# A two-layer decoder on one core: small norm operations and Newton steps change engine, ternary weights are made in another layout, and some products are merged

## What is computed

```python
x = layernorm(x + decay_mix(x) + bias)                 # triangular decay matrix over 256 channels
x = layernorm(x + cross_attention(x, ctx))             # 16 heads, 64 context rows
x = layernorm(x + experts(x) + shared(x))              # top 1 of 8 experts
x = layernorm(x + spectral_attention(x))               # fft over heads, each normalised, cumulative sum
x = layernorm(x + latent_cross_attention(x, ctx))      # weights folded: Wq, w_kc_q, W_qr, W_kr; w_kc_kv, Wo
x = layernorm(x + ternary_ffn(x))                      # weights made ternary in groups of 64

def ternary_quant(w, g=64):
    w = w.astype(bfloat16); w_g = w.reshape(-1, g)
    scale = clip(mean(abs(w_g), -1), 1e-08)
    q = clip(round(w_g / scale), -1, 1)
    return w + ((q * scale).reshape(w.shape) - w)
```

## Time and profile before

| | |
|---|---|
| median of 3 runs | 691.98 us (689.49 to 692.77) |
| the profiled execution | 693.77 us, its span 692.5 us |
| instructions | 14605 |
| TensorE, VectorE, ScalarE, POOL busy | 590.3, 506.3, 406.3, 362.0 us |
| mean granted TensorE clock | 0.938 |

### The profile page before, as it was taken

The page is one execution under the profiler, slowest core; times in us unless marked ns, Lnnn a source line. Parts: engine busy times, 40 slices in busy tenths (PEclk is TensorE's granted clock), DMA queues, the critical chain, the costliest instruction groups (busy, mean ns, idle before and its releaser), DMA issues.

```text
span 692.5 us, 14605 instructions
## 1 busy us (share of the span) xinstructions
PE 590.3 (85%) x5393; PEld 456.3 (66%) x5393; DVE 506.3 (73%) x1297; ACT 406.3 (59%) x914; POOL 362.0 (52%) x405
## 2 busy tenths in 40 slices
PE   3899989889689999935448789999988999999995
PEld 3566867668566566622126578898666777878885
DVE  2675667668667666757999878678698998968475
ACT  2667756767665454624534637665855666577474
POOL 2255345364753003269899894635654544256465
PEclk9899999999999999965867999999998999999998
DMA  6753221110535432441101010001100010000001
GB/s 190 211 162 107 55 92 48 52 41 2 168 117 166 142 104 84 123 151 50 40 25 56 1 32 1 2 1 31 32 26 6 1 31 3 1 1 2 1 1 62
DMA packets 50416, 41.98 MB, mean 61 GB/s; under 512 B 15513, under 2 KB 48794, under 8 KB 50330
## 3 DMA queue, kind: packets, MB, share of 16 engines
q1 hardware_dynamic: 48810, 36.85, 17.9%
q0 software_dynamic: 1536, 4.20, 1.9%
HBM read 31.72 MB, written 10.35 MB: 61 GB/s over the span
## 4 chain that ended last, share of the span: by engine, by line
PE 55%; DVE 21%; ACT 8%; issue 5%; SPq 4%; DMA 4%; POOL 3%; DVEq 0%; POOLq 0%
PE bank L1032 8%; PE bank L1034 8%; PE bank L1033 8%; PE bank L1039 7%; PE bank L1453 6%; SPq L858 4%; PE bank L1217 2%; PE bank L1120 2%; PE bank L1106 2%; DVE wide L1766 2%; DMA wide<-in_L_ffn_down_w 2%; ACT first L1592 1%; PE bank L1129 1%; PE bank L1318 1%; DVE wide L1869 1%
## 5 line engine op out<-in xcount | busy, mean ns | idle before, releaser
L1766 DVE TENSOR_TENSOR first<-bank,first 128x512 f16<-128x512 f32 (+3 forms) x141 | 75.6, 556 | 23.3 <-ACT first L1601 9.8
L1039 PE MATMUL bank<-c_identity,first 128*128 128x128 f32 (+2 forms) x353 | 60.0, 285 | 23.5 <-DMA first<-in_x 9.8
L2223 POOL TENSOR_TENSOR first<-first 128x512 f16<-128x512 f32 x44 | 51.2, 1164 | 42.7 <-ACT first L1653 35.8
L1039 PEld LDWEIGHTS bank<-c_identity,first 128*128 128x128 f32 (+2 forms) x353 | 39.7, 140 | 35.0 <-ACT first L1592 10.3
L1032 PE MATMUL bank<-wide,first 128*128 128x256 f16 (+3 forms) x199 | 55.8, 290 | 4.5 <-DVE first L1766 2.1
L1039 PE MATMUL bank<-c_identity,wide 128*128 128x128 f32 (+3 forms) x211 | 36.6, 297 | 26.1 <-POOL wide L2311 9.0
L1033 PE MATMUL bank<-wide,first 128*128 128x256 f16 (+3 forms) x199 | 55.8, 290 | 0.0
L1034 PE MATMUL bank<-wide,first 128*128 128x256 f16 (+3 forms) x199 | 55.7, 290 | 0.0
L2203 POOL TENSOR_TENSOR first<-first,minus_half 128x2 f32<-128x2 f32 x30 | 22.2, 739 | 55.5 <-DVE first L1875 55.5
L1039 PEld LDWEIGHTS bank<-c_identity,wide 128*128 128x128 f32 (+3 forms) x211 | 24.7, 147 | 33.1 <-POOL wide L2311 10.1
L2258 POOL TENSOR_TENSOR wide<-wide 128x768 bf16<-128x768 bf16 x8 | 13.5, 1685 | 61.1 <-DVE wide L1862 61.0
(11 more groups left out here) (469 smaller groups left out, 2160.0 us busy)
## 6 DMA issues: line engine op xcount, KB each, us to landing
first<-sent_rows SPq DMA_DIRECT2D x20, 128.0 KB, 2.0
made_rows<-first SPq DMA_DIRECT2D x20, 128.0 KB, 1.9
wide<-in_L_xattn_Wq SPq DMA_DIRECT2D x9, 256.0 KB, 3.1
wide<-in_L_ffn_gate_w SPq DMA_DIRECT2D x8, 256.0 KB
wide<-in_L_ffn_up_w SPq DMA_DIRECT2D x8, 256.0 KB
wide<-in_L_ffn_down_w SPq DMA_DIRECT2D x8, 256.0 KB
wide<-in_L_xattn_Wo SPq DMA_DIRECT2D x16, 128.0 KB
wide<-in_L_ffn_w_gate_up SPq DMA_DIRECT2D x8, 256.0 KB
```

Source lines behind the costliest of these rows:

```text
L1039: last = nc.tensor.transpose(view[0:m, c0:c0 + n], src, kc["identity" if dt == F32 else "identity_bf"][0:n, 0:n])
L1766: return V.tensor_tensor(lo, whole, hi, ALU.subtract)
L2223: G.tensor_tensor(B.pl[r], B.pf, B.ph[r], ALU.subtract).then_inc(says("ex_l"), 1)
```

## The change

- `ln` keeps only the statistics. Minus the mean, variance plus eps, the pow and the shift are all on POOL in `ln_pow`; `ln_x` only applies them.
- `nr` keeps the two integer operations; a new part `nr_x` on POOL does the three Newton steps with four operations each.
- The ternary weights: `f_16` writes the two-byte copy with the 12 groups side by side (`of_groups`), so the group's scale is a repeated row of 12. `f_sc` has one operation less and makes two edges; `f_gt` compares with tensor_tensor and subtracts; `f_q` is one VectorE part of three operations, the last of which writes the original order.
- `hb` puts two heads in the two halves of the partitions and alternates them; `krT` is block diagonal over 128 rows, so `hc` has one product for two heads, and `hk` is one transpose. The bias is one product over 128 rows, two of which hold its high and low part. `ss` folds the two halves, so `rm` has half the products.
- The plan has new lengths and `settle` makes 30 passes instead of 8.

```diff
     def norm(u, n, rank, summed="res"):
-        p.add("ln", u, n, "DVE", 131, [(summed, u, n)], rank)
-        p.add("ln_pow", u, n, "POOL", 71, [("ln", u, n)], rank)
-        p.add("ln_x", u, n, "ACT", 120, [("ln_pow", u, n)], rank)
+        p.add("ln", u, n, "DVE", 108, [(summed, u, n)], rank)
+        p.add("ln_pow", u, n, "POOL", 95, [("ln", u, n)], rank)
+        p.add("ln_x", u, n, "ACT", 85, [("ln_pow", u, n)], rank)
...
-            p.add("f_sc", 0, i, "DVE", 160, [("f_16", 0, i)], rank)
-            p.add("f_gt", 0, i, "DVE", 183, [("f_sc", 0, i)], rank)
-            for n2 in range(4):
-                p.add("f_q", 0, 4 * i + n2, "POOL", 164, [("f_q", 0, 4 * i + n2 - 1) if n2 else ("f_gt", 0, i)], rank)
+            p.add("f_sc", 0, i, "DVE", 170, [("f_16", 0, i)], rank)
+            p.add("f_gt", 0, i, "DVE", 155, [("f_sc", 0, i)], rank)
+            p.add("f_q", 0, i, "DVE", 195, [("f_gt", 0, i)], rank)
...
-        p.add("nr", u, 0, "DVE", 355, [("ft_n", u, 0), ("ft_n", u, 1)], k)
-        p.add("nr_k", u, 0, "DVE", 81, [("nr", u, 0), ("ft_raw", u, 0), ("ft_raw", u, 1)], k)
-        p.add("nr_q", u, 0, "POOL", 106, [("nr", u, 0), ("ft_raw", u, 0), ("ft_raw", u, 1)], k + 0.1)
+        p.add("nr", u, 0, "DVE", 60, [("ft_n", u, 0), ("ft_n", u, 1)], k)
+        p.add("nr_x", u, 0, "POOL", 350, [("nr", u, 0)], k)
+        p.add("nr_k", u, 0, "DVE", 81, [("nr_x", u, 0), ("ft_raw", u, 0), ("ft_raw", u, 1)], k)
+        p.add("nr_q", u, 0, "POOL", 106, [("nr_x", u, 0), ("ft_raw", u, 0), ("ft_raw", u, 1)], k + 0.1)
...
-    p.settle(8, 8)
+    p.settle(8, 30)
...
-        flip(bank("hk", 0, j), [(n * DC, R, W.kr[:, n, :]) for n in range(HEADS)]).then_inc(says("hk"), 1)
+        flip(bank("hk", 0, j), [(0, P, W.kr.rearrange("p h n -> p (h n)"))]).then_inc(says("hk"), 1)
...
-        for n in range(HEADS):
-            for q in range(2):
-                last = mm(b[0:R, n * D:(n + 1) * D], W.qr[:, q, n, :], k.t1[:, n, q, :], start=(q == 0), stop=(q == 1))
+        for q in range(2):
+            for n in range(HEADS):
+                last = mm(b[n * R:(n + 1) * R, 0:D], W.qr[:, q, n, :], k.t1[:, n, q, :], start=(q == 0), stop=(q == 1))
...
-            for n in range(HEADS):
-                mm(b[:, (2 * c + n) * DC:(2 * c + n + 1) * DC], k.t2[:, n * D + c * P:n * D + (c + 1) * P], k.krT[:, n * DC:(n + 1) * DC],
-                   start=True, stop=True)
+            mm(b[:, c * P:(c + 1) * P], k.t2[:, c * P:(c + 1) * P], k.krT, start=True, stop=True)
...
-                    for half in range(2):
-                        last = mm(o, kc["all_ones"][0:1, :], k.bias[half], start=False, stop=(half == 1))
+                    last = mm(o, kc["all_ones"], k.bias, start=False, stop=True)
...
-            for n in range(2):
-                last = mm(b[:, t:t + 1], B.ss[:, n * S + t * P:n * S + (t + 1) * P], k.one, start=(n == 0), stop=(n == 1))
+            last = mm(b[:, t:t + 1], B.ss[:, t * P:(t + 1) * P], k.one, start=True, stop=True)
...
-        fn(W.w16, W.raw, ACT.Copy).then_inc(says("f_16"), 1)
+        fn(of_groups(W.w16), W.raw.rearrange("p (g n) -> p g n", n=GRP), ACT.Copy).then_inc(says("f_16"), 1)
...
-        for t in range(T):
-            last = fn(B.shift[:, t:t + 1], B.mean[:, t:t + 1], ACT.Copy, scale=B.rstd[:, t:t + 1])
-        act.step(last)
...
+        dve.step(V.tensor_reduce(W.sc32, of_groups(W.w16), AX.X, ALU.add, apply_absolute_value=True))
+        dve.step(V.tensor_scalar(W.sc16, W.sc32, 1.0 / GRP, 1e-8, ALU.mult, ALU.max))
+        for n in range(2):
+            last = V.tensor_scalar(W.edge[n], W.sc16, 0.5 - n, None, ALU.mult)
...
+        V.tensor_tensor(by_row(W.qa), by_row(W.w16), each_group(W.edge[0]), ALU.is_gt)
+        dve.step(V.tensor_tensor(by_row(W.qb), by_row(W.w16), each_group(W.edge[1]), ALU.is_lt))
+        V.tensor_tensor(W.qa, W.qa, W.qb, ALU.subtract).then_inc(says("f_gt"), 1)
...
+        dve.step(V.tensor_tensor(by_row(W.qa), by_row(W.qa), each_group(W.sc16), ALU.mult))
+        dve.step(V.tensor_tensor(W.qb, W.qa, W.w16, ALU.subtract))
+        V.tensor_tensor(W.raw16.rearrange("p (g n) -> p g n", n=GRP), of_groups(W.w16), of_groups(W.qb), ALU.add).then_inc(says("f_q"), 1)
...
-        G.tensor_tensor(B.rstd, B.rstd, k.minus_half, ALU.pow).then_inc(says("ln_pow"), 1)
+        G.tensor_scalar(B.mean, B.mv[:, :, 0], -1.0, None, ALU.mult)
+        pool.step(G.tensor_scalar(B.rstd, B.mv[:, :, 1], EPS, None, ALU.add))
+        pool.step(G.tensor_tensor(B.rstd, B.rstd, k.minus_half, ALU.pow))
+        G.tensor_tensor(B.shift, B.mean, B.rstd, ALU.mult).then_inc(says("ln_pow"), 1)
...
+        for n in range(3):
+            pool.step(G.tensor_tensor(tmp, y, y, ALU.mult))
+            pool.step(G.tensor_tensor(tmp, tmp, x, ALU.mult))
+            pool.step(G.tensor_scalar(tmp, tmp, -0.5, 1.5, ALU.mult, ALU.add))
+            last = G.tensor_tensor(y, y, tmp, ALU.mult)
```

More of the change, by code:

```diff
@@ L609, in program @@
     k.w_fp = sb("w_fp", [P, FH // P, D], BF16)[:]
-    k.bias = pair("bias", [1, D])
+    k.bias = sb("bias", [P, D], F16)[:]
     k.slot_of = sb("slot_of", [P, NW])[:]
@@ L673, in program @@
     pre.dv = wide.tile([2])
-    pre.bias = wide.tile([S], F32, 1)
+    pre.bias, pre.rest = wide.tile([S], F32, 2), wide.tile([S], F32, 2)
     pre.ones32 = wide.tile([P])
@@ L1545, in hk_c @@
         act.wait_ge(*done("hk", 0, j))
-        fn(k.krT, bank("hk", 0, j)[0:R, 0:HEADS * DC], ACT.Copy).then_inc(says("hk_c"), 1)
+        act.wait_ge(*done("pm_pow", 0))
+        for n in range(HEADS):
+            own = slice(n * R, (n + 1) * R)
+            last = fn(k.krT[own, n * DC:(n + 1) * DC], bank("hk", 0, j)[own, 0:DC], ACT.Copy)
+        last.then_inc(says("hk_c"), 1)
     def ha_c(u, j):
@@ L1559, in hb_c @@
         act.wait_ge(*done("hb", 0, j))
-        fn(k.t2, bank("hb", 0, j)[0:R, :], ACT.Copy).then_inc(says("hb_c"), 1)
+        fn(k.t2, bank("hb", 0, j)[:, 0:D], ACT.Copy).then_inc(says("hb_c"), 1)
     def hq_hi(u, j):
@@ L1872, in ln @@
             last = V.bn_aggr(B.mv[:, t, :], B.stats[:, t, :])
-        dve.step(last)
-        V.tensor_scalar(B.mean, B.mv[:, :, 0], -1.0, None, ALU.mult)
-        V.tensor_scalar(B.rstd, B.mv[:, :, 1], EPS, None, ALU.add).then_inc(says("ln"), 1)
+        last.then_inc(says("ln"), 1)
     def turn_lo(u, n):
@@ L2117, in nr @@
         dve.step(V.tensor_scalar(tmp.bitcast(I32), x.bitcast(I32), 1, None, ALU.logical_shift_right))
-        dve.step(V.tensor_scalar(y.bitcast(I32), tmp.bitcast(I32), -1.0, float(0x5F3759DF), ALU.mult, ALU.add))
-        for n in range(3):
-            dve.step(V.tensor_tensor(tmp, y, y, ALU.mult))
-            dve.step(V.scalar_tensor_tensor(tmp, tmp, -0.5, x, ALU.mult, ALU.mult))
-            last = V.scalar_tensor_tensor(y, tmp, 1.5, y, ALU.add, ALU.mult)
-            if n < 2:
-                dve.step(last)
-        last.then_inc(says("nr"), 1)
+        V.tensor_scalar(y.bitcast(I32), tmp.bitcast(I32), -1.0, float(0x5F3759DF), ALU.mult, ALU.add).then_inc(says("nr"), 1)
     def nr_k(u, g):
         B = lane(u)
-        dve.wait_ge(*done("nr", u))
+        dve.wait_ge(*done("nr_x", u))
         for t in range(T):
@@ L2190, in pm_b @@
     def pm_b(u, g):
-        pool.step(G.tensor_copy(k.bias[0], pre.bias))
-        G.tensor_tensor(k.bias[1], pre.bias, k.bias[0], ALU.subtract).then_inc(says("pm_b"), 1)
+        rows = k.bias[0:2, :]
+        pool.step(G.memset(k.bias, 0.0))
+        pool.step(G.tensor_copy(rows, pre.bias))
+        pool.step(G.tensor_scalar(pre.rest, rows, kc["identity"][0:2, 1:2], None, ALU.mult))
+        G.tensor_tensor(rows, pre.bias, pre.rest, ALU.subtract).then_inc(says("pm_b"), 1)
     def eg_lo(u, e):
@@ L2329, in ss @@
             pool.wait_ge(*done("ss", u, g - 1))
-        G.tensor_tensor(B.ss, B.ss, B.s1, ALU.add).then_inc(says("ss"), 1)
+        last = G.tensor_tensor(B.ss, B.ss, B.s1, ALU.add)
+        if g == 3:
+            pool.step(last)
+            last = G.tensor_tensor(B.ss[:, 0:S], B.ss[:, 0:S], B.ss[:, S:2 * S], ALU.add)
+        last.then_inc(says("ss"), 1)
     def rm_pow(u, g):
@@ L2335, in rm_pow @@
         G.tensor_tensor(B.inv, B.inv, k.minus_half, ALU.pow).then_inc(says("rm_pow"), 1)
-    parts = {f.__name__: f for f in (pm_pow, pm_b, eg_lo, ln_pow, kv_bd, ex_l, rk_send, gt, f_q, rope, kd_lo, nr_q, nk_lo, cs_v, hs_lo, hf_lo, ss, rm_pow)}
+    parts = {f.__name__: f for f in (pm_pow, pm_b, eg_lo, ln_pow, kv_bd, ex_l, rk_send, gt, rope, kd_lo, nr_x, nr_q, nk_lo, cs_v, hs_lo, hf_lo, ss, rm_pow)}
     for name, u, g in k.plan.order["POOL"]:
```

86 lines of the change are left out of this document (40 added, 46 removed).

## The result

The changed kernel takes 705.34 us (median of 4 runs, 701.67 to 706.30), the kernel before took 690.82 beside it: ratio 1.0197, with a 95% interval of [1.0157, 1.0237] (intervals stand in brackets like this from here on). I had forecast 666 us in a range of 653 to 685. It is slower, and outside the range.

A forecast was written before the change was run, and what follows sets the result against it. TensorE bounds outside 300 to 400 us, VectorE behind POOL's long operations inside. Terms of -7, -13 and -7 us total -27 from the profiled 693.8, less 1.8 to the median: 666 us, range 653 to 685.

The forecast's parts named there:

- the sum: Whole kernel: -7 us up to 300, -13 in 300 to 400, -7 from 400, total -27, giving 666 us.
- The reading of the bound: TensorE bounds outside 300 to 400 us; inside, VectorE stands behind POOL's long operations, some 22 us of waiting.
- Two signs that I had named: POOL in 300 to 400 us falls from 88% to under 70%; first gathered rows to first gu some 10 us shorter.
- Part 1, ternary: Ternary weights: POOL loses 6.5 us a tile; VectorE goes from 3.4 to 5.2 us a tile, at worst 7.3.
- Part 2, Newton: Newton steps: VectorE loses 2.4 us a unit, 10 us in 300 to 400; twelve POOL operations take 5.0 us.
- Rival D: Newton's steps starve on POOL behind VectorE's two-input passes: nr_x takes 13.3 us, the kernel 716 us; chance 0.05.
- in 500 to 600 it is 2.6 us later, with the other three lanes as cover: Unit's Newton latency from 500 to 600 us rises by 2.6 us, hidden by other lanes; uncovered, eight units cost 21 us.
- Part 3, norms: 48 norms: small operations move to POOL, adding 0.75 us each; latency stays, VectorE is spared 1.6 us in 300 to 400.
- Part 4, products: Fewer TensorE products: eight folds save 10.4 us, bias 1.8, rm 4.2; of 12.2 us before 300, 60% counts.
- the sign of being wrong: Idle time of TensorE appearing in 0 to 300 us where folds were cut would show the forecast wrong.
- Part 5, the plan: Plan laid anew with other lengths and 30 passes may shift each engine's order: taken 0, bounded at +-6 us.
- Rival C: New order is worse or the lanes gain nothing; folds' gain stays, the rest is eaten: 686 to 695 us; chance 0.10.

The follow-up runs named there:

- Newton alone: The kernel before with only the Newton steps moved to POOL, every other order kept: 711.76 us, ratio 1.0286.
- the 681 us kernel: The changed kernel with f_16 reading permuted and writing in order, and the norms' small operations back on VectorE and ScalarE, its order kept: 680.71 us, ratio 0.9774.

## Why the prediction was wrong, point by point

Three terms stood at nothing in the sum and weren't nothing: `f_16`'s permuted write (11 us), what the norms' added work does to POOL's queue (12 to 18 us), and the new order (orders of one work lie up to 34 us apart).

*The reading of the bound* (TensorE outside 300 to 400 us, VectorE behind POOL within). The rows were right, the conclusion half right. Relief of VectorE by Newton's steps did bring 13 us in one order, and L1874's disturbed executions are gone with the line. But POOL at 88% was read as a nuisance to VectorE, not as a bound of its own. Newton alone lifted nothing there, because it went onto the fuller queue: 0.0286 slower. Two signs that I had named came out against the forecast: POOL in the middle stretch was to fall under 70% and fell to 72, and the stretch from the first gathered rows to the first `gu` product, which was to be 10 us shorter, was 6.5 longer (116.2 us for 109.7, from the first `res` of layer 1 at 326.8 and 311.5).

*Part 1, ternary.* The passes in order: taken about 0.5, measured 0.56 us. POOL's passes are gone. Two steps failed. First, "ACT's `f_16` writes permuted; I price that at nothing up to +0.3 us a tile, hidden behind ACT's 56% idle time": it was +2.8 us, and 0.56 of idle time on the average from 300 to 400 us is no cover in the experts' stage, where copies on ScalarE are awaited. Price shown: 11 us. No row of before had a two-byte write with a step from element to element, so the bound should have been wide; I took the row in order and called it near. Second, the passes that read with a step were 1.51 and 1.65 us for 0.95 and 0.5 to 0.95: the tile takes about 6.7 us of VectorE (1.51 + 0.65 for the three small ones, as before, + 5 x 0.57 + 1.65) where I took 5.2, within my bound of 7.3. The Trainium skill (Vector Engine (DVE) Microarchitecture Reference, Measured stream behaviour on trn2) states for four-byte elements that VectorE keeps its full rate only where a stream comes in pairs of adjacent words, and loses it where it hops at every element. VectorE's reduction agrees for two-byte ones (1.51 us with a step, 0.95 in order). On ScalarE the write was the dearer side by far.

*Part 2, Newton.* Price of `nr_x` 5.0 us: measured 4.4 undisturbed, and up to 6.6 in the middle stretch of after. Rival D's starving did not happen: no `nr_x` came near the 9.5 us from which it would have decided. Its forecast of 716 us was near the 711.8 of Newton alone, but by another mechanism (a full queue, and the longer latency), so this is no confirmation. Of the step "in 500 to 600 it is 2.6 us later, with the other three lanes as cover" the lateness was right, and the cover failed once in the old order, by 2.45 us.

*Part 3, norms.* This step failed most dearly. "The norm's latency then stays" was right, for a free norm (1.59 and 1.70 us) and on the average of all 48 in the old order (2.77 and 2.84), though less so in the new one (3.03 and 3.31); and yet the part costs 12 to 18 us. The missing term is POOL's queue: 48 norms at my own price of 0.75 us are 36 us more work on it (33 measured), and the sum has no term for what stands behind them.

*Part 4, products.* On TensorE the sizes were right. Eight products of `hb` and four of `hc` in a fold of after:

```profile
46.66 1.08 PE L1127 MATMUL bank<-wide 96*64 96x256 f32 x8
48.46 0.61 PE L1135 MATMUL bank<-krT,wide 128*128 128x128 f32 x4
```

1.1 and 0.6 us against 1.2 and 0.55 forecast; TensorE's total fell by 15.4 where 12 to 17 was named. Their value was 2 us in the old order (interval -0.5 to +4) and 12 in that of the 681 us kernel; I had taken 11. In the changed kernel TensorE idled instead, which I had named as the sign of being wrong. From 100 to 140 us it was busy 30.6 us in place of 34.5, and its granted clock was 0.87 in place of 0.96. The kernel of 681 us has 0.87 there too, so this stretch does not set the loss apart. How much of the loss is the clock I can't separate from the waits.

*Part 5, the plan.* "No row prices this; I bound it at +-6 us, taken 0." This is the other failed step. Four orders of one work spread over 34 us. By them a bound of +-17 was called for, and with it no chance of 0.87 for faster.

*The sum.* It has a slip of its own: 666.8 less 1.8 is 665, not 666. Forecast to result is about 40 us: the permuted write 11, the norms 12 to 18. Undoing both took the ratio from 1.0197 to 0.9774, which is more than the whole loss against the kernel before. The rest, 11 to 17 us, is within what orders do, and I have no run that assigns it further. Rival C, the new order is worse and the lanes gain nothing, was the nearest in kind and stopped at 695.

## What to carry to other kernels

Price work that is moved onto an in-order queue by what stands in that queue at that moment, ahead of it and behind it, not by its latency in a free one: three operations of 0.2 to 0.3 us in each of 48 norms cost 12 to 18 us in both orders, though a norm in a free queue took 0.1 us longer at most. When each engine's order is laid by a search, test an edit in a held order, in the old one and in the new, and put the scatter between orders into the range before anything else. And an access pattern is part of an instruction's price: put the step on the side and the engine where a row shows it to be cheap.

## What the runs showed of the hardware

A 128x768 fp32 to bf16 copy on ScalarE took 0.84 us in order, 1.53 us with the fp32 read at a step of 256 bytes, and 3.61 us with the bf16 write at a step of 24 bytes. VectorE's two-byte tensor_tensor over 768 columns took 0.56 us in order, also where one operand is a row of 12 numbers read 64 times over; 0.95 us where it is 12 numbers, each read 64 times in a row; and 1.54 us (median) with both inputs at a step of 24 bytes. VectorE's two-byte reduction over the same columns took 0.95 us in order and 1.51 with that step. A tensor_scalar of two columns takes 0.22 us on POOL where VectorE takes 0.17, and 0.26 us on the average of the changed kernel.
